# Layers 1 and 2 of a four-layer kernel in one block, group by group, with the last quad's division and addition behind layer 2's first scores

## What is computed

```
x = x + L0(_gn(x))   # 1x1 conv, group norm, a mixture of bases, 1x1 conv
x = x + L1(_gn(x))   # state-space mixer
x = x + L2(_gn(x))   # attention
x = x + L3(_gn(x))   # deformable 3x3 conv

# L1, per image (u of 64 channels, 256 pixels)
zxbcdt = einsum(x, W_in); z, xBC, dt = split(zxbcdt)
dt  = softplus(dt + dt_bias)
xBC = silu(depthwise_conv3x3(xBC) + conv_b); xs, Bm, Cm = split(xBC)   # 128, 16, 16
KV  = einsum(Bm, xs * (dt * exp(A_log)))
y   = (einsum(Cm, KV) + xs * D) * silu(z)                              # 128 channels
y   = (y - mean(y)) * rsqrt(var(y) + 1e-5) * ln_g + ln_b
out = einsum(y, W_out)                                                 # 64 channels

# L2, per image: 8 heads of 8 channels, 256 x 256 scores
q, k, v = proj(Wq), proj(Wk), proj(Wv)
out = softmax(q k^T / sqrt(8)) v, projected by Wo
```

## Time and profile before

| | us |
|---|---|
| median of 3 timed runs | 558.86 (557.93 to 560.33) |
| the profiled execution's own time | 554.14 |
| its span in the trace | 552.3 |
| PE, DVE, ACT, POOL busy | 413.1, 354.1, 289.6, 102.6 |
| granted TensorE clock, mean | 0.874 of full speed |
| DMA | 34.35 MB, mean 62 GB/s |

### The profile page before, as it was taken

How to read it: one execution, slowest core, us unless ns; L and a number is a source line. 1 busy time by engine, 2 the same in 40 slices (tenths; PEclk the granted TensorE clock), 3 DMA queues, 4 the chain that set the end, 5 groups by cost and what they waited for, 6 DMA issues and landing times. The chain is left out here.

```text
span 552.3 us, 9028 instructions
## 1 busy us (share of the span) xinstructions
PE 413.1 (75%) x3218; PEld 207.1 (37%) x3218; DVE 354.1 (64%) x670; ACT 289.6 (52%) x509; POOL 102.6 (19%) x106
## 2 busy tenths in 40 slices
PE   1326671599999528488779999955449999999995
PEld 1114551245454314223224444423324544455442
DVE  4447786323375697987559999342256878778784
ACT  1459974132423316147448888831646758486441
POOL 3500004000000003511001222110003717246000
PEclk9856995599999977759779999986858999999998
DMA  5400000800000001833500000009656091652302
GB/s 137 113 0 1 0 0 0 171 19 1 0 1 1 0 0 46 255 102 117 158 17 2 4 4 2 2 0 190 161 113 144 15 228 16 150 110 52 79 2 76
DMA packets 22649, 34.35 MB, mean 62 GB/s; under 512 B 5377, under 2 KB 17873, under 8 KB 21841
## 3 DMA queue, kind: packets, MB, share of 16 engines
q1 hardware_dynamic: 19920, 29.67, 22.2%
q10 hardware_dynamic: 2688, 4.16, 3.2%
HBM read 16.80 MB, written 4.64 MB: 39 GB/s over the span
## 5 line engine op out<-in xcount | busy, mean ns | idle before, releaser
L876 DVE TENSOR_REDUCE L_mx<-L_ring 128x2 f32<-128x512 f32 x128 | 82.3, 686 | 22.8 <-PE L_ring L993 22.0
L1259 DVE TENSOR_TENSOR L_s<-L_row_ps,L_cols 128x1024 f32<-128x1024 f32 x72 | 87.7, 1219 | 8.3 <-PE L_row_ps L1390 6.7
L931 ACT ACTIVATE L_e<-L_ring 128x512 f32<-128x512 f32 x128 | 74.2, 597 | 34.9 <-PE L_ring L1006 32.9
L1411 PE MATMUL L_acc<-L_s,L_t_sb 128*64 128x256 f32 x576 | 79.7, 398 | 1.1 <-DVE L_s L1259 1.0
L1320 ACT ACTIVATE L_cols<-L_col_ps 128x512 f32<-128x512 f32 x72 | 42.9, 597 | 45.2 <-PE L_col_ps L1398 44.9
L1006 PE MATMUL L_ring<-stacks_q_st,stacks_k_st 64*128 64x256 bf16 x256 | 49.5, 290 | 10.3 <-DMA stacks_q_st<-L_m_parts 10.3
L993 PE MATMUL L_ring<-stacks_k_st,stacks_q_st 64*128 64x256 bf16 x256 | 52.3, 305 | 6.2 <-DMA stacks_k_st<-L_k_parts 5.7
L1411 PEld LDWEIGHTS L_acc<-L_s,L_t_sb 128*64 128x64 f32 x576 | 35.5, 138 | 35.2 <-DVE L_s L1259 21.2
L1390 PE MATMUL L_row_ps<-L_hats,L_sel 48*128 48x512 bf16 x144 | 44.5, 391 | 0.0
L1029 PE MATMUL L_ctx_ps<-L_e,L_v_x 128*32 128x256 f32 x512 | 43.1, 411 | 0.0
L1381 PE MATMUL L_acc<-all_w_all,L_xn 64*128 64x192 f32 x96 | 26.3, 356 | 13.9 <-DVE L_t_sb L1239 13.9
(11 more groups left out here) (250 smaller groups left out, 747.1 us busy)
## 6 DMA issues: line engine op xcount, KB each, us to landing
L_hats<-L_parts SPq DMA_DIRECT2D x32, 216.0 KB, 5.0
L_hat<-L_offsets SPq DMA_DIRECT2D x24, 192.0 KB, 4.5
stacks_q_st<-L_q_parts SPq DMA_DIRECT2D x24, 128.0 KB, 3.1
L_mask<-L_offsets SPq DMA_DIRECT2D x12, 192.0 KB, 4.7
L_q_parts<-L_parts SPq DMA_DIRECT2D x8, 192.0 KB, 3.0
L_k_parts<-L_parts SPq DMA_DIRECT2D x8, 192.0 KB, 3.2
stacks_k_st<-L_k_parts ACTq DMA_DIRECT2D x12, 128.0 KB, 4.1
stacks_k_st<-L_k_parts SPq DMA_DIRECT2D x12, 128.0 KB, 2.7
```

The lines of the kernel that those rows point to most:

```text
L876: dve.tensor_reduce(mx[:, n % 2, :, head], ring[:, step % 3].rearrange("p (q s) -> p q s", q=2), AX.X, ALU.max).then_inc(max_read, 1)
L931: act.activation(e[:, k], ring[:, 3 + v % 3], ACT.Exp, scale=HD2 ** -0.5).then_inc(e_ready, 1)
L1259: dve.tensor_tensor(s[:, q], row_ps[:, q], cols[:, t % 3:t % 3 + 1].broadcast_to([P, 2, 2 * N]), ALU.mult).then_inc(s_ready, 1)
L1411: mm = pe.matmul(acc[C * e:C * e + C, b, 0:N], t_sb[:, b, h, (KK * e + t) * C:(KK * e + t + 1) * C], s[:, q, h, e * N:(e + 1) * N], start= ...
```

## The change

Layers 1 and 2 become one function, `layers12`, with one program for each engine; the end of layer 1's block and the norm of all pairs go. Layer 2's front part is done group by group, in places between the instructions of later quads and between the rows of layer 2:

- The norm has one instance for each group (`gns[g]`, 2 columns), split in `aggregate`, `variance`, `add_eps` and `shift_in`. The Sqrt on ACT and the reciprocal on DVE become one power of -0.5 on POOL (`invert`).
- The normalised copy `xn` is made by ACT (`norm`, Identity with a scale and a shift) and not by DVE. The second part of q and k (subtraction and cast) is made by POOL and not by DVE. There is room for two groups' parts, no longer for four.
- PSUM is shared: the ring of the maxima and its bank count of three stay; the scores have two banks until step 48 and three from there on (`score_bank`). Groups' projections go through one bank (`way`).
- The loads of group 0 are all on SP's queue, those of q of group 1 on ACT's. One store stands between two maxima on SP, or one load.
- The last quad's division and addition (`over_deviation(3)`, `add(3)`) stand in row 2 of layer 2.
- SP's and DVE's loops over groups and quads are written out.

The core of the diff (kept to the new order; helpers that only changed their name are left out):

```
-    def __init__(self, mem, signals, name, avg, mean, spread, of_x=0):
+    def __init__(self, mem, signals, name, avg, mean, spread, of_x=0, pairs=slice(0, NP)):
...
+    def invert(self, pool, minus_half):
+        pool.wait_ge(self.signals.var_ready, self.turn)
+        pool.tensor_tensor(self.scale[:], self.sp[:], minus_half[:, 0:1].broadcast_to([P, self.n]), ALU.pow).then_inc(self.signals.sd_ready, 1)
...
+    ROWS = range(FIRST - LAG, 8 * (B + 2))      # FIRST = 8: eight steps of largest stand in the last quad
+        way = lambda g: banks[:, 7 if g < 2 else 6, :]
+        score_bank = lambda v: 4 + v % 2 if v < THIRD_BANK else 4 + (v - THIRD_BANK) % 3   # THIRD_BANK = 48
...
+            # gpsimd
+                gns[0].invert(pool, minus_half)
+                for s in range(2):
+                    take_rest(0, s); take_mid(0, s); take_last(0, s)
+                gns[1].invert(pool, minus_half)
+                take_rest(1, 0); take_mid(1, 0); take_last(1, 0)
+                for n in range(B):
+                    split_maxima(n)
+                    spread_values(n)
+                    if n == 0: gns[2].invert(pool, minus_half); take_rest(1, 1); take_mid(1, 1); take_last(1, 1)
+                    if n == 1: take_rest(2, 0); take_mid(2, 0)
+                    if n == 2: gns[3].invert(pool, minus_half); take_last(2, 0); take_rest(2, 1)
+                    if n == 3: take_mid(2, 1); take_last(2, 1)
...
+            # vector, in the rows
+                    if u == 2:
+                        over_deviation(3)
+                        add(3)
+                        gns[3].aggregate(dve)
+                    if u == 14: take_values(2)
+                    if u == 16: gns[3].variance(dve)
+                    if u == 17: gns[3].add_eps(dve)
+                    if u == 20: shift_in(3)
...
+            # scalar, in the rows
+                    if u == -7: act.wait_ge(added, NQ - 1); deviation(NQ - 1); load_stacks(act, 1, 0)
+                    if u == -2: norm(2); take_first(2, 0)
+                    if u == 4: take_first(2, 1)
...
+            # tensor
+                turn_xs(3)
+                pe.wait_ge(v_all_ready, 1)
+                gns[1].send_mean(pe)
+                sum_kv(3)
+                gns[1].send_spread(pe)
+                send_y(3)
+                for k in range(6):
+                    largest(k)
+                    if k == 2:
+                        project(1, 0)
+                center_y(3)
+                project(1, 1)
+                largest(6)
+                largest(7)
+                send_o(3)
+                send_var(3)
+                project_values(1)
```

More of the change, by code:

```diff
@@ L144, in vector, with variance @@
         dve.sem_inc(on.stats_ready, 1)
-        dve.wait_ge(on.mean_ready, turn)
+        on.own_steps = step.n
+    def variance(self, dve):
+        on = self.signals
+        step = Steps(dve, on.own, on.own_steps)
+        dve.wait_ge(on.mean_ready, self.turn)
         step(dve.tensor_tensor(self.d[:], self.mv[:, :, 0], self.mean, ALU.subtract))
@@ L148, in vector, with add_eps, shift_in @@
         dve.tensor_tensor(self.var[:], self.sp[:], self.mv[:, :, 1], ALU.add).then_inc(on.sp_ready, 1)
[L149 to L152 removed]
+        on.own_steps = step.n
+    def add_eps(self, dve):
+        dve.wait_ge(self.signals.spread_ready, self.turn)
+        dve.tensor_scalar(self.sp[:], self.spread, EPS, None, ALU.add).then_inc(self.signals.var_ready, 1)
+    def shift_in(self, dve, bias=None, gamma=None, beta=None, inverted=False):
+        on = self.signals
+        step = Steps(dve, on.own, on.own_steps)
+        dve.wait_ge(on.sd_ready, self.turn)
+        if not inverted:
+            step(dve.reciprocal(self.scale[:], self.sd[:]))
         if gamma is not None:
@@ L574, in _, with add @@
-                quad(0, first=True)
-                with dve.Fori(1, NQ - 1) as q:
-                    quad(q)
-                quad(NQ - 1, last=True)
-                over_deviation(NQ - 1)
-                add(NQ - 1)
+                def add(q):
+                    x_quad = x[:, 2 * q:2 * q + 2, :]
+                    dve.scalar_tensor_tensor(out=x_quad, in0=sd[:], scalar=b_out[:], in1=x_quad, op0=ALU.add, op1=ALU.add).then_inc(added, 1)
+                    dve.wait_ge(added, q + 1)
+                    for h in range(2):
+                        dve.bn_stats(signals.x_bn[:, 2 * q + h, :], x[:, 2 * q + h, :]).then_inc(signals.x_stats, 1)
@@ new lines, in _ @@
+                copy_b(0)
+                take_v(0)
+                take_kv(0)
+                take_y(0)
+                copy_o(0)
+                take_var(0)
+                copy_b(1)
+                take_v(1)
+                take_kv(1)
+                take_y(1)
+                over_deviation(0)
+                copy_o(1)
+                add(0)
+                take_var(1)
+                gns[0].aggregate(dve)
+                copy_b(2)
+                gns[0].variance(dve)
+                take_v(2)
@@ new lines, in _ @@
+                gns[0].add_eps(dve)
+                take_kv(2)
+                shift_in(0)
+                take_y(2)
+                over_deviation(1)
+                copy_o(2)
+                add(1)
+                take_var(2)
+                gns[1].aggregate(dve)
+                weights.wait(dve, 2)
+                take_values(0)
+                copy_b(3)
+                take_v(3)
+                gns[1].variance(dve)
+                take_kv(3)
+                gns[1].add_eps(dve)
@@ new lines, in largest @@
+                def largest(step):
+                    n, k = divmod(step, 8)
+                    h, p = k % 2, k // 2
+                    if step == 0:
+                        pe.wait_ge(acts_ready, 2 * NQ)
+                    if step % 32 == 0:
+                        pe.wait_ge(stacked[step // 32], LOADS * 16)
+                    if step > 2:
+                        pe.wait_ge(max_read, step - 2)
+                    for q in range(2):
+                        mm = pe.matmul(banks[:, step % 3, q * N:(q + 1) * N], rows_of(q_st, n, h, p)[:, q * P:(q + 1) * P], rows_of(k_st, n, h, p),
+                                       start=True, stop=True)
+                    mm.then_inc(max_ps, 1)
@@ L1064, in _ @@
+                project_values(1)
+                for u in ROWS:
+                    c, k = divmod(u, 8)
+                    if u + LAG < 8 * B:
+                        largest(u + LAG)
+                    if 0 <= u < 8 * B:
+                        scores(u)
                     if k == 0 and image_of(c - 2):
```

845 lines of the change are left out of this document (475 added, 370 removed).

## The result

| | before | after |
|---|---|---|
| median, us | 558.39 (553.44 to 560.33, 4 runs) | 539.31 (536.32 to 545.1, 4 runs) |
| the profiled execution's own time | 554.14 | 536.32 |
| its span | 552.3 | 534.5 |

The ratio of after to before is 0.9653, 95% interval 0.9564 to 0.9742. I forecast 539.3 for the median and 534.5 for the profiled execution: the first was met, the second missed by 1.8 us. That the median was met so closely is luck. I took it to lie 4.7 us above the profiled execution, as before, and in after it lies 3.0 above. The steps under the sum were less good than the sum.

What follows compares the result with a forecast made beforehand. PE bound layer 1's quads, DVE led in the changeover, both together bound the image loop. First scores 21.2 us earlier, less 1.5 given back in the loop, left 19.6: 558.86 - 19.6 = 539.3 us, range 529 to 551.

Steps and rivals of the forecast that it cites:

- the signs that I gave for being right: Landmarks expected, among them quad 3 2 to 2.5 us late, image 0's scores at 219 to 223, power under 1.5 us.
- Step 1: Last quad's start: group 0's projections move into PE-bound quad 2, so it starts 2.2 us late, at 186.2.
- Step 2: Group 0's stack in the last quad: complete at 197.4, with PE waiting 5 us for it at `largest(0)`.
- Step 3: First row of layer 2's order: PE ready at 211 including 2 us for a low clock, DVE at 212.3.
- Step 4: Image 0's scores: at 221.6, 21.2 us earlier than before, taking ACT's own rate for its six DMA issues.
- Step 5: Layer 2's images 0 to 14: 108.2 us against 106.7 before, so 1.5 of the gain go back.
- two banks and the clock: Images 0 to 14: 1.5 us over 48 steps for two score banks, 1 for a lower clock behind image 2's wait.
- The division: Last quad's division and addition, 5.65 us, now stand in image 0: work moved, not removed.
- A: Rival, more gained: PE's clock stays up, ACT issues at SP's rate, POOL is fast; gain 27, 532 us; chance 0.22.
- B: Rival, half given back: low PE clock and two banks cost images 0 to 6 1.5 us each; 550; chance 0.16.
- C: Rival, slower: POOL's power of P us costs some 4 P - 5 more; about 566 at 8 us; chance 0.07.
- D: Rival, chain moves whole: last quad hangs some 20 us behind group 0's stack, nothing gained, 558; 0.05 with other evens.

Runs made afterwards that it cites:

- e5: Kernel before, with layer 1's loops over quads written out on DVE and ACT: median 555.36 us, ratio to before 0.9973.
- e6: Changed kernel with SP issuing group 0's stores of q and k ahead of the loads of q and k: median 539.10 us.
- e11: Changed kernel with the last quad's `y` on DVE ahead of layer 2's first three reductions: median 537.83 us.
- e16: Changed kernel with e4's and e11's edits and 14 unused products in PE's wait for group 0's stack: median 534.49 us.
- e14: Changed kernel with the edits of e4, e6 and e11 together, without unused products: median 535.77 us.
- e7: Changed kernel with each group's power of -0.5 on POOL done four times: median 544.23 us.
- e3: Changed kernel with group 2's q and k projections sent later on PE, q's in row 1 instead of row -2: median 539.29 us.
- e18: e16 with 35 more unused products in PE's waits around image 0: median 530.06 us.
- e2: Changed kernel with two banks for the scores to the end, the third never coming: median 540.48 us.
- e4: Changed kernel with group 3's power on POOL moved behind the maxima of image 3: median 534.33 us.
- e1: Changed kernel with the last quad's division, addition and statistics in row -7, ahead of image 0's first scores, instead of row 2: median 539.74 us.

## Why the prediction came out, step by step

The sum came within 1.8 us because errors of both signs met in it: the first scores came 1.3 us earlier than forecast, and images 0 to 14 took 2.9 us longer. All times here are of the profiled executions. Of the signs that I gave for being right, two were missed: `largest(0)` went at 194.38 and not at 196 to 199, and PE's wait for the stack was 3.77 us and not 4 to 6.

**Step 1** held. The last quad starts 184.60 (forecast 186.2). Relative to quad 2 the fillers cost 2.4 us (forecast 2.2). What I missed is the 1.7 us by which quad 2 starts earlier. Of these, 1.0 lie between quad 0 and quad 2, where ACT's table load and the written-out loops give that much (e5), a part of the diff that I had priced at nothing. The rest was there before quad 0.

**Step 2** put the stack at 197.4 and the wait at 5 us; measured 194.38 and 3.77. Its own rows give 197.1 (the last load starts at 194.4, and 2.7). The 3.0 us are the 1.7 of step 1, that slip, and on SP 3.41 and 3.54 us from store to load where I took 3.96 from a stretch in which other DMAs ran. POOL's power was 0.69 to 0.71 us (taken 0.8), its cast 0.61 (0.7), the two sets of parts 3.2 and 3.7 us (3.5 each). But the wait was not all that held the last quad: 1.3 us less of it took 0.8 off S and nothing off D (e6), while y, which needs no stack and stood behind the reductions, took 2.6 off S (e11).

The Trainium skill ("GPSIMD Engine Reference", "1. Specifications") names DVE instructions with two SBUF inputs as those that contend with POOL. The trace agrees: POOL's subtraction took 1.44 us at 178.37, beside DVE's product of two SBUF tensors, and 1.15 at 215.48; there DVE's shift of 128x2, with two SBUF inputs too, took 0.90 instead of the 0.16 that it took at 192.84, with POOL idle. By that rule I had the stack 1 us earlier; it was earlier for the reasons above, not that one.

**Step 3** forecast the rows' start 212.3, measured 208.86. Less the 3.0 of step 2 the rest is right to 0.4. In it I took 3.3 us for `y`, whose four instructions measured 2.6. The 2 us for the clock lie between the 1.2 and the 2.9 that e16 shows against e11 and e14.

**Step 4** is the one that failed in its mechanism while its number held (221.6, measured 220.29). I made ACT's six DMA issues the limit. They were done at 212.5, 3.8 us long, and ACT then waited for the shift:

```profile
209.25 3.26 ACTq L571 DMA_DIRECT2D stacks_q_st<-L_q_parts  x5
216.74 1.09 ACT L946 ACTIVATE L_xn<-all_x,L_gn_shift,L_gn_scale 128x256 f32<-128x256 f32 x2 [7.32 <-DVEq L790]
```

The limit is group 2's norm, whose parts stand in rows -8 to -3 of DVE between reductions. I had priced it at its instructions (1.4 us) and not at its hand-overs: from the addition of quad 2 (DVE, 207.42) to q it is 10.5 us. PE's mean was done at 210.84 and DVE took it up at 212.24, and PE's spread was done at 213.42 and taken up here:

```profile
214.60 0.15 DVE L168 TENSOR_SCALAR L_gn_sp<-L_banks 128x2 f32<-128x2 f32 x1
215.75 0.90 DVE L183 TENSOR_TENSOR L_gn_shift<-L_gn_d,L_gn_scale 128x2 f32<-128x2 f32 x1
```

Each of these two hand-overs thus stood behind DVE's rows for 1.4 and 1.2 us. From the rows' start to the scores I had 9.3 us by ACT's queue, and it took 11.4. e7 shows that the norm is the limit, since 2.0 us more of power delay the scores by 2.0, and e3 shows that moving its consumer alone gives nothing in the end. PE's low clock is the smaller part: e18 holds it at 1.00 from the rows to image 0, and that stretch falls from 12.7 to 11.3 us, 0.9 of it in q. That the hand-overs make the rest is read from the timeline; no run takes DVE's rows out from between them.

**Step 5** forecast 108.2 us from image 0 to 14, measured 111.1. Images 1, 2, 4 and 5 were 8.2, 11.0, 8.4 and 6.8 (forecast 8.0, 11.2, 8.7, 7.1). Mis-sized were image 0 (12.1 for 9.8) and image 3 (10.8 for 7.7), against 2.5 us that I had set aside for two banks and the clock; the banks' 1.5 were not there at all (e2). Image 3 is the clock behind image 2's wait: forecast 1 us, and e4, which takes the wait away, gives back 1.3. The other 1.7 remain with the clock at 1.00, where image 3 takes 9.4. I take them for the stack, q and other extra work of that image, for which I had put 1.05 over the steady 6.65; no run separates them. Image 0 is not settled. Where products kept the clock up for most of it (0.61 in 220 to 224, 0.96 to 1.00 around), it fell from 13.0 to 11.9 (e16 to e18), still 2.1 above the forecast. DVE's pieces of division, addition and statistics measured 5.8 us (forecast 5.65). A table load of ACT for the exponents (1.28 us) and PE's wait for them (0.96 in after, 1.48 in e18) stand in it too; no run isolates them.

**The division** "moved, not removed": shown by e1, its late place is worth 0.8 us of D against row -7.

Of the rivals, A had two of its three conditions (ACT at SP's rate, POOL fast) and neither decided; its clock that stays up came only where products held it, and was then worth 1.2 us of S (e11 to e16) and 2.3 of D more (e16 to e18). B's low clock was there, its banks were not. C did not occur, but its mechanism is real: its rule of 4 P - 5 gives 5.8 us for e7's P of 2.7, where D grew by 5.3, though not by its shares; at 0.7 it gives nothing. D did not occur.

The gain itself, 22.5 us at the first scores, is read from the landmarks. What the parts of the change give singly (a norm for each group, `xn` on ACT, the second parts on POOL, the spread stores and loads) no run isolates; the runs isolate only the late division and, in the kernel before, the written-out loops.
